# The low part of an expert's down weights: made on GpSimd in place of VectorE

## The reference

```python
gu = jnp.einsum('th,ehf->tef', flat, gate_up_proj) + gate_up_bias
gate = jnp.minimum(gu[..., :I], LIMIT)
up = jnp.clip(gu[..., I:], -LIMIT, LIMIT)
glu = gate * jax.nn.sigmoid(gate * ALPHA)
act = (up + 1.0) * glu
down = jnp.einsum('tei,eih->teh', act, down_proj) + down_bias
out = jnp.einsum('teh,te->th', down, w)
```

## Time and profile before

| what | value |
|---|---|
| median of 3 runs | 1678.53 us (1676.74 to 1679.24) |
| the profiled execution, as a run | 1680.17 us |
| its span, first to last instruction | 1678.5 us |
| mean granted clock of PE | 0.976 of full speed |
| busy over the span: PE, PEld | 95%, 69% |
| busy over the span: DVE, ACT, POOL | 78%, 41%, 50% |
| expert stage | about 953 us to the end |

### The profile page before, as it was taken

The page is one execution under the profiler, slowest core; times in us unless marked ns, Lnnn a source line. Parts: engine busy times, 40 slices in busy tenths (PEclk is TensorE's granted clock), DMA queues, the critical chain, the costliest instruction groups (busy, mean ns, idle before and its releaser), DMA issues. The chain is left out here.

```text
span 1678.5 us, 30420 instructions
## 1 busy us (share of the span) xinstructions
PE 1587.3 (95%) x9607; PEld 1165.3 (69%) x9607; DVE 1309.5 (78%) x2477; ACT 694.2 (41%) x1316; POOL 836.8 (50%) x628
## 2 busy tenths in 40 slices
PE   5898999999999999999998799979999999999996
PEld 4554555565555555655553589879999999999995
DVE  4576777878878778787786589888888889888885
ACT  3254544545445446454445233343334233333331
POOL 3355656566666676666678413222332333333332
PEclk9899999999999999999999799989999999999998
DMA  6343434343543534434334724644646356354442
GB/s 223 83 112 84 112 96 108 107 111 89 120 105 106 103 100 108 115 82 115 95 89 72 208 70 151 203 137 132 191 152 195 96 157 191 108 166 139 132 130 97
DMA packets 112246, 209.48 MB, mean 125 GB/s; under 512 B 32400, under 2 KB 33808, under 8 KB 112080
## 3 DMA queue, kind: packets, MB, share of 16 engines
q1 hardware_dynamic: 91248, 144.73, 31.8%
q0 software_dynamic: 20640, 62.49, 12.6%
q10 hardware_dynamic: 192, 0.26, 0.0%
HBM read 204.33 MB, written 37.51 MB: 144 GB/s over the span
## 5 line engine op out<-in xcount | busy, mean ns | idle before, releaser
L872 DVE TENSOR_REDUCE negmax<-max_ps 128x2 f32<-128x1024 f32 x252 | 306.8, 1217 | 142.3 <-PE max_ps L599 136.8
L730 ACT ACTIVATE pt<-work 128x512 f32<-128x512 f32 x512 | 277.5, 594 | 258.8 <-PE work L611 250.1
L1111 POOL TENSOR_TENSOR acc<-acc,pt 128x1024 f32<-128x1024 f32 x128 | 303.8, 2377 | 116.0 <-ACT pt L730 115.8
L1108 POOL TENSOR_TENSOR acc<-pt 128x1024 f32<-128x1024 f32 x64 | 153.4, 2398 | 183.6 <-PE work L631 112.3
L599 PE MATMUL max_ps<-ks,qs 96*128 96x512 f32 x504 | 194.4, 467 | 21.0 <-DVE negmax L872 13.4
L1600 ACT ACTIVATE sig<-gate 128x256 f32<-128x256 f32 x156 | 65.0, 417 | 289.5 <-DVE gate L1660 273.1
L1492 PE MATMUL gu_ps<-xgT_hi,early_wg_hi 128*128 128x256 f32 x640 | 179.8, 281 | 1.5 <-DVE xgT_lo L1652 1.5
L1492 PE MATMUL gu_ps<-xgT_lo,early_wg_hi 128*128 128x256 f32 x640 | 177.9, 278 | 0.0
L1492 PE MATMUL gu_ps<-xgT_hi,early_wg_lo 128*128 128x256 f32 x640 | 177.7, 278 | 0.0
L611 PE MATMUL work<-qs,ks 98*128 98x512 f32 x512 | 169.8, 411 | 4.7 <-DMA qs<-m_lo 3.9
L1492 PE MATMUL gu_ps<-xgT_hi,wg_hi 128*128 128x256 f32 x608 | 170.6, 281 | 0.0
(11 more groups left out here) (297 smaller groups left out, 3675.8 us busy)
## 6 DMA issues: line engine op xcount, KB each, us to landing
early_raw_g<-w_gate_up SPq DMA_DIRECT2D x39, 2048.0 KB
early_raw_d<-w_down SPq DMA_DIRECT2D x20, 1024.0 KB
raw_d<-w_down SPq DMA_DIRECT2D x19, 1024.0 KB
qs<-q_hi SPq DMA_DIRECT2D x252, 64.0 KB
ks<-k_hi SPq DMA_DIRECT2D x252, 64.0 KB
bd<-b_down SPq DMA_DIRECT2D x39, 256.0 KB
x_in<-x SPq DMA_DIRECT2D x36, 256.0 KB, 3.2
ctxT_raw<-ctx_t SPq DMA_DIRECT2D x32, 256.0 KB, 3.7
```

The lines of the kernel that those rows point to most:

```text
L730: e.activation(pt[k % 2][:, h, :], in_work("exp", u, k, h)[:, :], ACT.Exp, scale=scale).then_inc(exped.sem, 1)
L872: e.tensor_reduce(negmax[:, u % 2, n:n + 2], pair_of(u, r)[:, :, :], AX.X, ALU.max, negate=True).then_inc(maxed.sem, 1)
L1108: e.tensor_tensor(acc[:, heads, :], pt[0][:, heads, :], pt[1][:, heads, :], ALU.add).then_inc(added.sem, 1)
L1111: e.tensor_tensor(acc[:, heads, :], acc[:, heads, :], pt[k % 2][:, heads, :], ALU.add).then_inc(added.sem, 1)
```

## The change

GpSimd makes the low part of the down weights, between `store_sums(i-1)` and `fetch_sums(i)`, for tile i+1. It waits for all four chunks of `wd_hi`, reads the tile's flag and branches. The last tile's stays on VectorE, with its flag. In all other tiles VectorE has neither the two `down_lo` steps nor the flag's read.

```diff
@@ on_dve
                 if i >= 1:
                     mix(i - 1)
-                down_changed = changed_flag(e, now)
+                if now == n_tiles - 1:
+                    down_changed = changed_flag(e, now)
                 e.wait_ge(bg_in[now % 2], turn(now) * 16)
...
                         if i + 2 < n_tiles:
                             gate_up_lo(i + 2, KD // 2 + f, changed)
-                    else:
+                    elif now == n_tiles - 1:
                         down_lo(now, f - 2, down_changed)
@@ on_pool
+            def down_lo(i):
+                s = i % 2
+                e.wait_ge(wd_hi_made[s], turn(i) * KF)
+                with e.If_ne(changed_flag(e, i), 0):
+                    for k in range(KF):
+                        d_lo(e, s, k)
+                with e.Else():
+                    e.sem_inc(wd_lo_made[s], KF)
...
             for i in range(-1, n_tiles):
                 if i + 3 < n_tiles:
                     fetch(i + 3)
                 if i >= 1:
                     store_sums(i - 1)
+                if i + 1 < n_tiles - 1:
+                    down_lo(i + 1)
+                if i >= 1:
                     fetch_sums(i)
```

## The result

The changed kernel takes **1723.78 us** (median of 6 runs, 1713.97 to 1731.14) beside 1679.2 for the kernel before in the same session (6 runs): ratio 1.0251, 95% interval 1.0231 to 1.027, so 2.5% slower. (The ratios in this document are the recorded ones with their intervals. They are not exactly the quotients of the medians, which is 1.0265 here.) The direction and the mechanism are the forecast's; the size is not: 1705 was forecast. The median passes 1722, the end of the range, by 1.8 us; as a ratio it lies just inside, as 1722 is 1.0259 times the 1678.53 from which the forecast started. Lines behind L1968 have moved by one: the sums are now gathered in L2021 and scattered in L2026.

A forecast was written before the change was run, and what follows sets the result against it. PE bounds the kernel, with VectorE close behind by a head start of 1.9 to 2.8 us; 32.6 late, less 2.8 head start and 3 early gain, gives +27: 1707 for such an execution, median 1705 us, range 1690 to 1722.

The forecast's parts named there:

- main term: GpSimd's queue: sums gather behind the subtractions, 11.6 us from wd_hi to landing, so mix starts 3.9 us later.
- Nine tiles: New-expert tiles 8, 12, 13, 17, 18, 24, 25, 30, 34 make VectorE later: 8 x 3.9 + 1.4 = 32.6 us.
- Rival (a): GpSimd's lock on VectorE, not the gather, sets mix's delay: 2.4 us late, +14 us, 1693; chance 0.12.
- (c): VectorE's lead decides: mix delayed under 0.4 us a tile, PE never waits, 3 to 5.5 us faster, 1674; chance 0.05.
- (d): No change: delay about 1 us a tile eats the early gain, or gather leaves early; within 3 us, 1678; chance 0.07.
- the 1.4 counted: Delay at tile 8, counted as a third because the head start is large and VectorE soon waits for PE.
- free, with 2.5 us to spare: Tiles without a new expert: gathers land at about 1451.6, before the mix at 1454.08, so no cost.
- rival (b): Gathers also late in the 21 expert-keeping tiles after tile 8, from costly flag and branch or slow landings: 1715 up; chance 0.10.
- I take 3 us of gain: Tiles 0 and 1, no gather behind: VectorE gains 5.5 us less its waits for GpSimd; ends 0 and 5.5.
- tile 7, which was to cost nothing: In tiles 5 and 7 mix already came 11.5 us after wd_hi; 11.6 against 11.5, nothing.
- The head start of 2.8 us: VectorE's lead over PE at tile 37, absorbing the first part of the delay: 32.6 - 2.8 = 29.8 us.
- I count nothing: PE's granted clock may fall after its new waits; costed at nothing, since PE then waits for VectorE anyhow.

The follow-up runs named there:

- gather-first run: Changed kernel with GpSimd fetching tile i's sums before making wd_lo of tile i+1, subtractions still on GpSimd: 1686.28 us, ratio 1.0028 to the kernel before.
- flag-first run: Changed kernel with GpSimd reading the flag first and waiting for wd_hi only where the expert is new: 1711.09 us, ratio 1.0168 to the kernel before.
- two-tile run: Changed kernel with only tiles 0 and 1 on GpSimd, VectorE doing the rest as before: 1682.23 us, ratio 1.0008 to the kernel before.
- half run: Changed kernel with GpSimd making two of the four chunks and VectorE the other two: 1704.13 us, ratio 1.0144 to the kernel before.

## Why the prediction was right, and where its size was off

**Right.** The direction, the mechanism and its main term. Nine tiles were to have 11.6 us from `wd_hi` to mix; they have 11.14 to 12.38, mean 11.63. Summed over their periods the nine are 33.3 us longer, against 32.6 forecast. The terms inside moved against each other: 0.75 for flag and branch (0.6), 5.60 for subtractions with collisions (5.14 + 0.8), 1.44 for the issues (1.58), 3.56 for the landing (3.52). The gather-first run shows that the queue is the cause. Rival (a), the lock as the thing that decides, has its collisions (3.05 us a tile), but they lie inside the gather's delay; alone, without the late gather, they would have left +0.28%. Rivals (c) and (d) are out. That the sum of the nine comes out within 0.7 us is in part luck: the landings in them took 3.2 to 4.6 us, not 3.52, tile 8 was 2.4 us late for the 1.4 counted, and others were less late than 3.9.

**Wrong, by about 13 us.** The sum gave +27 for such an execution, the trace has +40.4 (1720.6 against 1680.17). Four terms:

1. "free, with 2.5 us to spare": the gathers of tiles that keep their expert. This step failed. It counted a calm landing of 3.52 us, but the later issue falls beside SyncE's weight loads in some tiles, where mix starts 6.4 to 7.2 us after it. Mixes 13, 14, 32 and 36 are 7.3 us late together. That is rival (b) in its second form (slow landings), in four tiles and not in 21, and it comes on top of the sum. The flag-first run takes most of it back.
2. "I take 3 us of gain": there is none. Mix(0) is 0.7 us later than before, mix(6) 1.2 (it waits 2.08 us for its gather, in tile 7, which was to cost nothing): some 4 us off the sum. The step granted VectorE 5.5 us less its waits for GpSimd, and the collisions were bounded by one GpSimd operation each. One of VectorE's waited out four (5.5 us). As mix(0) moves by some microseconds from one execution to the next, it is the two-tile run's median that shows this: no gain.
3. The clock behind PE's last waits. The head start of 2.8 us is there: mix(36) is 41.5 us later, the last `down(37)` starts 38.2 later, so 3.3 are absorbed, and 0.5 go back in a second wait, for the second half of the sums. But those 24 matmuls take 7.67 us instead of 5.49; less the 0.5, that is 1.7 us of slower matmuls. The step that failed is "I count nothing" for the clock, with the reason that PE waits for VectorE anyhow; in the last tile VectorE waits for PE.
4. The nine tiles, 33.3 for 32.6: +0.7.

7.3 + 3.7 to 4.2 + 1.7 + 0.7 make 13.4 to 13.9, where 13.4 are to be explained. Three smaller readings were off and move the sum little: the last of VectorE's three shorter waits for PE lies at 1643.8, not at 1158; PE's starts taken from the earlier trace rows are about 0.16 us late, so the head starts are that much shorter; and the four subtractions hold VectorE for 2.43 us, not 2.74.

PE's `down(37)` in the changed kernel, some of its 24 matmuls, and the clock by stretches (length, busy us per engine, granted clock, DMA share, GB/s):

```profile
1681.79 0.47 PE L1532 MATMUL d_ps<-wd_hi,hid_hi 128*128 128x512 f32 x1 [3.62 <-DVE acc L1695]
...
1683.24 0.76 PE L1532 MATMUL d_ps<-wd_hi,hid_hi 128*128 128x512 f32 x1 [0.51 <-DVE acc L1695]
...
1684.23 0.63 PE L1532 MATMUL d_ps<-wd_lo,hid_hi 128*128 128x512 f32 x1
1684.65 0.63 PE L1532 MATMUL d_ps<-wd_hi,hid_hi 128*128 128x512 f32 x1
...
1687.13 0.40 PE L1532 MATMUL d_ps<-wd_lo,hid_hi 128*128 128x512 f32 x1
```

```profile
1684.00:1685.00 1.00, 1.00 (x4) 0.79 (x3) 1.00 (x3) 0.42 (x1) 0.84 (x1) 0.50 0.70 262
...
1686.00:1687.00 1.00, 1.00 (x6) 0.82 (x5) 0.46 (x2) 0.42 (x1) 0.00 (x0) 1.00 0.64 242
```

PE has waited 3.62 us for the sums and 0.51 more for their second half, and then works until 1686 us at the lower of its two levels, 1.2 GHz (granted clock 0.50), with a matmul every 0.43 us; behind that it is back at 2.4 GHz (1.00), with one every 0.23. The same is seen behind the wait in tile 25 (0.66 from 1470 to 1473 us); there VectorE sets the pace, and the next mix is no later for it.

**What stays open.** Why the median exceeds the profiled execution (by 3.2 us; the kernel's runs spread over 17) was not looked into. That the loads are what slows the gather for mix(13) is read from the traces, late beside them in the change and calm ahead of them in the flag-first run; no run moved a load by itself. Landings of 4.2 to 6.1 us also occur in tiles with a new expert (half run, tile 12 the slowest), and what sets those is open.

## What to carry to other kernels

When compute is given to an engine that also issues gathers, look first at what stands behind it in that queue: here 2.7 us of operations given away cost 3.7 us a tile, because a gather that takes 3.5 us to land went out behind them, and putting the gather first took nine tenths of that away. Also ask what share of the removed work stood in waiting time (0.4 to 0.8 us of 2.4 here), and what the receiving engine does to the giver while it works; the collisions ate the rest. A wait that moves a DMA later must be checked in the tiles where the wait ends at once, too: there the DMA may meet a load that it used to miss.

## What the runs showed of the hardware beyond what I expected

- One subtraction of VectorE with two SBUF inputs was held for four GpSimd operations in a row (6.71 us instead of 1.22), and it had started, by the records, 0.64 us before the first of them. The forecast had allowed one GpSimd operation per collision. The Trainium skill, "SBUF — State Buffer", section "Who interferes with whom", says that whichever engine issues first gets the shared port pair and the other blocks for the instruction. These rows show a block longer than one instruction, and for the engine that started first by the records; but GpSimd was issuing a gather at that moment (958.40 to 959.35), so they don't show who had the ports.
- GpSimd pays little: a subtraction of 128x512 took 1.26 to 1.28 us at its shortest and 1.47 in the median, 0.2 more. VectorE paid 0.7 to 1.1 us per collision, on operations of 0.42 us.
- By the start of the mix that waited for it, a gather of 128 rows landed 3.5 us after its issue in a calm stretch, 3.2 to 4.6 us after it in the nine tiles of the changed kernel, and 6.4 to 7.2 us after it beside a weight load (mixes 13, 32, 36).
